# A pair of tiles as the unit of work in both layers of a two-layer graph network

## The reference

```
x: (12500, 64)   src, dst: (200000,), dst sorted   edge_attr: (200000, 32)
edge_type: (200000,) in 0..7   edge_weight: (200000, 1)

# layer 0
x_t  = leaky_relu(x @ W1n + b1n) @ W2n + b2n              # (12500, 64)
e_t  = leaky_relu(edge_attr @ W1e + b1e) @ W2e + b2e      # (200000, 64)
agg  = segment_sum(x_t[src] * e_t * dp_scale, dst)
h    = layernorm(x + agg * res_w) * gamma + beta
x    = layernorm(x + h)
# layer 1
rel_w = einsum('rb,bio->rio', w_comp, weight)             # (8, 64, 64)
xw    = einsum('ni,rio->rno', x, rel_w)
agg   = segment_sum(xw[edge_type, src] * edge_weight, dst)
x     = layernorm(x + relu(agg + h_bias))
```

## Time and profile before

| | us |
|---|---|
| median of 3 runs | 5263.4 (5251.9 to 5273.67) |
| profiled execution, its own time | 5280.59 |
| its span | 5278.8 |
| first gather of layer 0's loop, last gather of layer 0 | 165.1, 2894.0 |
| first and last gather of layer 1 | 2986.0, 5250.9 |

### The profile page before, as it was taken

The page is one execution under the profiler, slowest core; times in us unless marked ns, Lnnn a source line. Parts: engine busy times, 40 slices in busy tenths (PEclk is TensorE's granted clock), DMA queues, the critical chain, the costliest instruction groups (busy, mean ns, idle before and its releaser), DMA issues.

```text
span 5278.8 us, 48622 instructions
## 1 busy us (share of the span) xinstructions
PE 2470.4 (47%) x11571; PEld 1883.3 (36%) x11572; DVE 1627.0 (31%) x4106; ACT 563.1 (11%) x1305; POOL 2973.7 (56%) x3193
## 2 busy tenths in 40 slices
PE   6655555655565565565666523332333233333333
PEld 5544444444444443444444322222222222222223
DVE  4322223232232322332333323223332333333233
ACT  2111111111112121221122100000000000000000
POOL 4455555555544554454544266666666666666665
PEclk7667777676766676666666655556555555555555
DMA  3111111111111111111111111111111111111111
GB/s 91 24 30 30 30 30 29 42 29 39 32 40 38 29 42 39 38 41 38 28 51 37 38 23 23 23 23 25 23 25 23 25 25 25 26 25 25 25 27 24
DMA packets 201295, 169.13 MB, mean 32 GB/s; under 512 B 84565, under 2 KB 137036, under 8 KB 201060
## 3 DMA queue, kind: packets, MB, share of 16 engines
q0 software_dynamic: 100096, 102.60, 10.2%
q1 hardware_dynamic: 100082, 64.38, 4.0%
q10 hardware_dynamic: 882, 0.13, 0.0%
HBM read 134.80 MB, written 32.10 MB: 32 GB/s over the span
## 4 chain that ended last, share of the span: by engine, by line
issue 30%; another core or an unknown queue 21%; DVEq 17%; PE 17%; DVE 10%; ACT 3%; ACTq 0%; DMA 0%; POOL 0%; SPq 0%; POOLq 0%
DVEq L841 6%; DVEq L900 5%; DVE work L900 5%; PE ps_agg L1181 4%; PE ps_o L1173 3%; PE ps_z L1161 2%; DVEq L875 2%; PE ps_fin L1255 2%; PE ps_agg L1255 2%; DVEq L863 1%; DVE hid L912 1%; PE ps_T L1244 1%; DVEq L869 1%; ACT L576 1%
## 5 line engine op out<-in xcount | busy, mean ns | idle before, releaser
L521 POOL DMA_INDIRECT rows<-node_table,acc x1524 | 1437.8, 943 | 1329.9 <-DVE work L919 902.5
L521 POOL DMA_INDIRECT rows<-rel_table,row_ix x1564 | 1475.3, 943 | 881.6 <-issue 450.9
L900 DVE TENSOR_SCALAR work<-ps_x,rel,enorm 128x128 f32<-128x128 f32 x1564 | 558.0, 405 | 891.2 <-issue 815.3
L1169 PE MATMUL ps_o<-b2e,ones 3*128 3x256 bf16 x391 | 135.5, 346 | 1078.3 <-DVE hid L912 870.8
L1181 PE MATMUL ps_o<-work,rows 128*64 128x128 f32 x1248 | 273.4, 388 | 681.2 <-issue 349.0
L1181 PE MATMUL ps_agg<-work 128*64 128x128 f32 x3128 | 574.0, 343 | 35.1 <-issue 19.0
L860 DVE TENSOR_TENSOR acc<-acc,ps_agg 64x128 f32 x548 | 152.3, 278 | 1215.9 <-remote 814.1
L1181 PEld LDWEIGHTS ps_agg<-work 128*64 128x64 f32 x3128 | 456.2, 176 | 145.8 <-issue 140.5
L1181 PEld LDWEIGHTS ps_o<-work,rows 128*64 128x64 f32 x1248 | 218.5, 202 | 722.1 <-issue 378.3
L1169 PEld LDWEIGHTS ps_o<-b2e,ones 3*128 3x128 bf16 x391 | 37.5, 96 | 1185.8 <-DVE hid L912 923.1
L1181 PE MATMUL ps_agg<-work,rows 128*64 128x128 f32 x1256 | 264.8, 385 | 285.3 <-issue 160.3
(11 more groups left out here) (140 smaller groups left out, 1891.5 us busy)
## 6 DMA issues: line engine op xcount, KB each, us to landing
rows<-rel_table,row_ix POOLq DMA_INDIRECT x1564
attr<-in_edge_attr_dram SPq DMA_DIRECT2D x78, 320.0 KB
rows<-node_table,acc POOLq DMA_INDIRECT x1524
rel_table<-acc SPq DMA_DIRECT2D x13, 1792.0 KB
node_table<-work SPq DMA_DIRECT2D x24, 128.0 KB, 2.0
out_dram<-x_sb SPq DMA_DIRECT2D x13, 224.0 KB
rel_table<-acc SPq DMA_DIRECT2D x7, 256.0 KB
x_sb<-in_x_dram SPq DMA_DIRECT2D x1, 768.0 KB, 6.3
```

Of the source, the lines that this page charges most:

```text
L521: nc.gpsimd.indirect_dma_start(rows[0:n, slot_of(t), j, :], None, table, bass.IndirectOffsetOnAxis(ap=lists[0:n, t, j : j + 1], axis=0),). ...
L900: last = nc.vector.tensor_scalar(o[:, j, :], iota_ps, r[:, j : j + 1], weights[:, j : j + 1], ALU.is_equal, ALU.mult)
L1169: nc.tensor.matmul(ps_o[u % 2][:, 0 : J * F], ones_3[:], b2e_3[:], start=True, stop=False, skip_group_check=True)
```

## The change

The unit of work becomes a pair of tiles (`V = 2`), in both layers, on VectorE, ScalarE and TensorE. A loop trip holds two halves of five pairs, so 20 tiles where it held 10; `next_chunk` still stands once per ten tiles.

- One one-hot instruction, one message, one hidden layer, one copy and one lower branch serve two tiles.
- `sum_by_target` takes two message columns as stationary side (128 columns) and two one-hots as moving side (256 columns): two products per tile. Only the two diagonal blocks of the result are wanted; they lie on partitions 0 to 63 and 64 to 127. `add_window` adds each half to its own half of `acc` (two instructions per tile), and the transpose at the chunk's end adds the halves (`fold`).
- Layer 1 scales the gathered rows by the weights, in the same `message` as layer 0. The weights of ten tiles are staged by ScalarE in a PSUM bank (`stage_weights`). The one-hots are unweighted, the rings of five become rings of two, and the slot of a gather is free when the message is made.
- Waits compare with a register `lead` that is counted up once per step and serves all of the step's waits, since the semaphores start with leads (`MSG_LEAD`, ...). The gathers wait once per pair.
- The bias of W2e is copied by eight small DMAs, and the attributes are loaded ten tiles at a time.

```diff
+    V = 2
+    HALF = BODY // V
+    TURN = 2 * HALF
...
-            def add_window(first, bank):
-                a = acc[0:F, 0, bass.ds(first, P)]
-                return nc.vector.tensor_tensor(a, a, bank[0:F, 0:P], ALU.add)
...
+            def add_window(first, bank, at):
+                for g in range(2):
+                    f = slice(g * F, (g + 1) * F)
+                    a = acc[f, 0, bass.ds(first, P)]
+                    last = nc.vector.tensor_tensor(a, a, bank[f, at + g * P : at + (g + 1) * P], ALU.add)
                 return last
...
+            def add_sums(l, p, r):
+
+                if is_fixed(p) and p == LAST:
+                    dve.wait_ge(added[l], p + ADD_LEAD)
+                dve.wait_ge(scattered[l], count(p, 0, SUM_LEAD))
+                add_window(window_of(r, 0), sums[r], 0).then_inc(first_added[l], 1)
+                dve.wait_ge(first_added[l], count(p, 0, SUM_LEAD))
+                if width(p) == V:
+                    add_window(window_of(r, 1), sums[r], 2 * P).then_inc(added[l], 1)
...
+            def message(l, p, u):
+                w = width(p)
...
+                    dve.wait_ge(gathered[l][u % HALF], landed)
+                pair = rows[:, u % HALF * V : u % HALF * V + w, :, :].rearrange("p t j f -> p (t j) f")
+                if l == 0:
+                    dve.wait_ge(mm2_done, count(p, 0, MM2_LEAD))
+                    factor = ps_o[u % 2][:, 0 : w * J * F].rearrange("p (q f) -> p q f", f=F)
...
+                    factor = ps_o[u // HALF % 2][:, at : at + w * J].rearrange(
+                        "p (q o) -> p q o", o=1).to_broadcast([P, w * J, F])
+                nc.vector.tensor_tensor(msg[:, u % 2, 0 : w * J, :], pair, factor, ALU.mult).then_inc(msg_ready[l], 1)
...
+            def step(l, p, u):
+
+                if not is_fixed(p) or p + 1 <= LAST:
+                    prepare(l, p + 1, (u + 1) % TURN)
+                if l == 0 and (not is_fixed(p) or p + 2 <= LAST):
+                    edge_hidden(p + 2)
+                add_sums(l, p, u % 2)
+                extras(l, p, u % 2)
+                if not is_fixed(p):
+                    dve.reg_add(lead, lead, 1)
...
-            def weighted_hot(o, r, s):
-
-                weights = enorm[:, bass.ds(s, 1), :].rearrange("p o j -> p (o j)")
-                for j in range(J):
-                    last = nc.vector.tensor_scalar(
-                        o[:, j, :], iota_ps, r[:, j : j + 1], weights[:, j : j + 1], ALU.is_equal, ALU.mult)
...
-                if t >= BODY:
-                    pool.wait_ge((msg_ready, tile_done)[l], t + 1 - BODY)
+                if t >= BODY and t % V == 0:
+                    pool.wait_ge(msg_ready[l], (t - BODY) // V + 1 + MSG_LEAD)
...
+            def sum_by_target(data, hot, bank, at):
+                for jj in range(2):
                     last = nc.tensor.matmul(
-                        bank[0:F, 0:P], data[:, j, :], hot[:, j, :], start=(j == 0), stop=(j == J - 1)
+                        bank[:, at : at + 2 * P], data[:, 2 * jj : 2 * jj + 2, :], hot[:, 2 * jj : 2 * jj + 2, :],
+                        start=(jj == 0), stop=(jj == 1),
                     )
                 return last
...
+            def step0(p, u, i):
+                scatter(0, p, u % 2)
+                if not is_fixed(p) or p + 2 <= LAST:
+                    edge_second(p + 2, u)
+                if not is_fixed(p) or p + 3 <= LAST:
+                    edge_first(p + 3)
+                if not is_fixed(p) or p + 4 <= LAST:
+                    attr_transpose(p + 4, (u + 4) % TURN, i + (u + 4) // TURN)
+                if not is_fixed(p):
+                    pe.reg_add(lead, lead, 1)
...
+            for q in range(V * J):
+                sp.dma_start(b2e_3[:, q * F : (q + 1) * F], b2e_parts[:, :, :]).then_inc(s_b2e3, 16)
```

More of the change, by code:

```diff
@@ L841, in span_of, with count @@
+            x_done, shift, left, lead, landed, staged = (
+                dve.alloc_register(f"dve_{n}") for n in ("x_done", "shift", "left", "lead", "landed", "staged")
+            )
+            def count(p, ahead, offset):
+                return p + 1 + ahead + offset if is_fixed(p) else lead
+            def span_of(p, r):
                 dve.reg_load(
[L842 to L844 removed]
@@ new lines, in half, with layer @@
+            def half(l, k, h, first, finish_chunk):
+                for u in range(HALF):
+                    step(l, first + u, h * HALF + u)
+                    if u == NORM_AFTER:
+                        next_chunk(dve, done, limit, k, finish_chunk)
+                dve.sem_inc(half_done[l], 1)
+            def layer(l, finish_chunk):
+                dve.reg_mov(done, 0)
+                dve.reg_mov(x_done, 0)
+                dve.reg_mov(lead, 3)
+                dve.reg_mov(landed, PAIR_GATHERS)
+                dve.reg_mov(staged, 1)
+                prepare(l, 0, 0)
+                with dve.Fori(0, LOOPS) as i:
+                    for h in range(2):
+                        half(l, i * 2 + h, h, i * TURN + h * HALF, finish_chunk)
+                half(l, BODIES - 1, 0, LAST - HALF, finish_chunk)
+                step(l, LAST, HALF)
+                dve.sem_inc(half_done[l], 1)
+                remaining_chunks(dve, done, limit, finish_chunk)
@@ L1057, in _ @@
[L1057 to L1063 removed]
+            layer(1, finish1)
         @block.tensor
@@ new lines, in count, with attr_transpose @@
+            def count(p, offset):
+                return p + 1 + offset if is_fixed(p) else lead
+            def attr_transpose(p, u, turns):
+                if u % HALF == 0:
+                    pe.wait_ge(attr_loaded[u // HALF % 2], (turns + 1) * 16)
+                for t in range(width(p)):
+                    last = nc.tensor.transpose(
+                        ps_T[:, t * P : (t + 1) * P], attr[:, u // HALF % 2, u % HALF * V + t, :], ident[:])
+                last.then_inc(transposed, 1)
```

574 lines of the change are left out of this document (290 added, 284 removed).

## The result

| | before | after |
|---|---|---|
| median, us | 5268.53 (4 runs, 5251.9 to 5285.55) | 5323.55 (4 runs, 5311.19 to 5336.51) |
| profiled execution, its span | 5280.59, 5278.8 | 5311.19, 5309.3 |

After / before is 1.0105, 95% interval 1.0059 to 1.015. A second measurement gave 1.0094 (1.0067 to 1.0121). The forecast was 4530 us; the change makes the kernel 1% slower.

What follows compares the result with a forecast made beforehand. Instructions and gathers were taken to share one rate, stalling VectorE and TensorE above GpSimd's floor. Head 165 + layer 0 2305 + between 91 + layer 1 1955 + end 27 = 4543 us span, hence 4530; range 4300 to 4750.

Steps and rivals of the forecast that it cites:

- the cut in records and instructions: Both layers: PE records 36% down in layer 0; layer 1's engine instructions per pair from 42 to 22.
- GpSimd's pitch as the floor: Both layers: a gather every 1.25 us, 5.0 us per tile, so 1905 us for layer 0 and 1955 for layer 1.
- the loss comes once in some three steps: Layer 0 before: some 8.5 us lost once in three tiles, in a cycle of 19.6 us.
- Stalls, layer 0: Layer 0: one stall per 126 engine instructions, so one in 2.3 pairs after; 3.7 us per pair, before 5.7.
- Layer 1: Half the instructions cut the loss from 7.9 to about 4.1 us per pair; sum 8.4, so GpSimd sets the pace, 1955 us.
- The two windows of the earlier trace: Instructions and gathers draw on one rate: a gather worth 19 instructions, 17.1 per us in all; called no proof.
- its sign of being wrong: Layer 0's stall: the prediction is wrong if instructions set the stall's length, not its number.
- B: Layer 0: rarer instructions buy nothing because the stall grows with each one's work; layer stays 2730, time 4954 us; chance 0.17.
- C: Both layers: loss is a share of time, 43% in layer 0, 68% in layer 1; time 5432 us, slower; chance 0.08.
- A: Both layers: stalls short enough for the ring of ten tiles, so GpSimd sets the pace; time 4131 us; chance 0.20.
- D: Both layers' loops: the longer trip costs instruction fetches; 5270 us, or some 6400 with ten per trip; chance 0.10.
- Small terms: Outside the layers' loops: head 0 to 5 us more, between the layers 80 to 100, behind the last gather 20 to 30.

Runs made afterwards that it cites:

- e1: Kernel after with one gather per tile in place of four (sums not the reference's): 2610.63 us.
- e2: Kernel before with one gather per tile in place of four (sums not the reference's): 2695.29 us.
- e3: Kernel after with each pair's one-hots made twice, the first time into unused space: 5376.02 us; kernel before on that chip 5209.9.
- e10: Kernel after with a GpSimd memset of 256 columns (0.33 us), waited for, once a tile: 4313.93 us; kernel before on that chip 4073.77.
- e12: Kernel before with a GpSimd memset of 1024 columns (0.97 us), waited for, once a tile: 4790.22 us; unchanged on that chip 4073.77.
- e4: Kernel after with a GpSimd memset of 256 columns, waited for, ahead of every gather: 5033.63 us; kernel before on that chip 5209.9.
- e5: Kernel before with a GpSimd memset of 256 columns, waited for, ahead of every gather: 5021.46 us; unchanged on that chip 5283.4.

## Why the prediction was wrong

**Right:** the cut in records and instructions, GpSimd's pitch as the floor, that the loss comes once in some three steps with VectorE in a "remote" wait, and that GpSimd waits for messages in it.

**The step that failed: "Stalls, layer 0" and the loss in "Layer 1".** A stall was priced per instruction. By the prediction's own sum a pair in layer 0 has 7.0 us of work and 1.4 of chunks; measured are 2696 / 190.5 = 14.2 us, so the stall is 5.8 us a pair, against 3.7 forecast and 5.7 before. In layer 1 a pair takes 2281 / 195.5 = 11.7 us, less 4.2 of work: 7.5 us lost, against 4.1 forecast and 7.9 before. The loss hardly moved. The runs with one gather a tile give the work itself, chunks included: 6.95 us a pair in layer 0 and 5.07 in layer 1 (e1), 7.38 and 5.20 for two tiles (e2), at a higher granted clock (0.91 from 500 to 1200 us in both). The prediction had 8.4 and 4.2. So the work explains none of the 2.1 us a pair by which its sum for layer 0 was short, and at most 0.9 of the 3.3 in layer 1 (11.7 against 8.4).

The error began in the reading of the earlier trace rows. The products that the add waits for were taken to be those of 1567.45; they are those of 1563.53, over before VectorE began to wait, so that 9.06 us were lost and not some 8.5. And the wait was put down to instructions held up, though GpSimd's pause of 4.94 us, in the middle of which the wait ends, stood in the same stretch of the trace and was not laid beside it. The two windows of the earlier trace rows fitted two unknowns and so could not speak against it, as was said there; the test that could, whether "remote" waits end in GpSimd's pauses, was open in the trace of before (88 of the 88 adds of layer 0 that are over 5 us late do).

**Why half as many instructions gain nothing.** The loss is time during which a signal is held. In the three stretches above it ends 2.5 to 5.5 us after the end of GpSimd's unbroken run. With pairs, a slot's release, a step and a signal all cover twice the tiles: the pause frees twice as much ring, GpSimd runs twice as long on it, and the wait is twice as long. This is how the cycle came to be 38.5 us for three pairs where it was 19.6 for three tiles. The counts over the layers agree. GpSimd's waits for messages in layer 0 went from 134 of 6.2 us to 69 of 11.6 us, one for about 2.7 tiles and one for about 2.7 pairs; in layer 1 from 98 of 3.5 us to 44 of 7.6 us. The number of losses fell somewhat more than forecast (one in 2.7 pairs, 2.3 forecast), but their length doubled, which is what the prediction named as its sign of being wrong. Why the number of steps in a cycle stays the same is argued here, not shown by a run of its own, and the adds of layer 1 that are late in the middle of a run are not covered by it.

**The rivals.** B (layer 0 unchanged) has layer 0 right, 2696 against 2730, but let layer 1 fall to GpSimd's pace. C (a share of time is lost, slower) had the right sign and put the cost in layer 1's larger work for VectorE; e3 shows that extra work there costs an eighth to a quarter of itself. A (GpSimd's pace, 4131) is the picture that the paced kernels show. On a chip without lateness it should hold for the kernel after too, which never met one: e10 less 782 x 0.33 us gives 4056, and the same sum from e12 with 0.97 us gives 4032 for the kernel before, which measures 4075; so some 4100 us, an estimate. By it the change would be worth about nothing there, for before is at the floor already, and the forecast's 14% could come true on neither kind.

**D, fetching.** The instruction queue, the view of the earlier trace rows, moves in layer 0 (250 to 2900 us)

```profile
q14 instruction: 142, 1.16, 0.1%
```

where it was 12 packets: the longer loop does fetch again. The Trainium skill ("Runtime: NRT & Kernel Launch", section "Instruction fetch mechanics") states that a taken branch to a target out of the window forces a fetch before execution goes on; the packets agree with it. But e1 runs the same loop in 2610.63 us, less than e2's 2695.29 with the shorter one, and e4 runs at GpSimd's pace with it. No run shows a price for it.

**Small terms.** Head, 0 to 5 us forecast, +12.6 measured; between the layers 80 to 100, 113.8 measured; behind the last gather 20 to 30, 40.3 measured. In e4 the three are 149.6, 50.7 and 17.5 us, though the work in them is the same, and in e5, the kernel before with the same pause, 144.5, 42.0 and 16.9. Without lateness, then, the change adds 5.1, 8.7 and 0.6 us to them; the rest of what was measured is lateness too. As measured on the kernel after they make up for more than the whole of the difference of 30.5 us.

## What to carry to other kernels

When waits for a fast engine end at odd moments ("remote", or well after the record that releases them), look at what an unrelated engine does just then: here 46 of the 48 long ones in layer 0 ended in a pause of the engine that issues indirect gathers. Match each wait with the very product that it waits for, by the order of the steps and not by what lies nearest in time. Before pricing fewer or cheaper instructions, take away the suspected cause in the smallest way (one gather for four, a pause ahead of each) and see what the rest needs; here that is 2600 of 5300 us. And a larger unit of work lengthens a loss that lasts until a unit is released, so it can keep the whole loss with half the events (layer 0: 826 us in 134 waits of GpSimd, then 802 in 69).

## What the runs showed of the hardware

- With gathers issued every 1.25 us, TensorE's signals reach ScalarE and VectorE late, on four of six chips: in the stretch shown 28.5 us after the end of the product's record (4255.51 to 4284.01), and up to 37.0 us over the kernel after. Signals from VectorE and ScalarE to TensorE are not late there (at most 1.1 us). Whether the increment is late or the product itself finishes late can't be told from the records.
- A pause of 0.33 us ahead of each gather, or of 0.97 us ahead of every fourth, ends it; 0.11 or 0.17 us ahead of each, or 0.33 or 0.54 ahead of every fourth, only lessens it.
- On the other two chips the same kernel before takes 4073.77 and 4075.63 us, 22% less. A time on one chip, or a ratio, says nothing of the other kind here: e10's code is 3.2% faster than the kernel before on the one and 5.9% slower on the other.
- Giving the busiest engine a third more to do (1018 us of memsets on 2988) made the kernel faster: 5033.63 us, where the kernel before took 5209.9 on the same chip and the kernel after 5323.55 on another.
